# In the last group's rows, GpSimd takes the last tile's deviation ahead of the second tile's result, and VectorE finishes the third tile

## The reference

```python
y = mixed + x                                     # the experts' weighted sum, and the residual
mu = jnp.mean(y, axis=-1, keepdims=True)
var = jnp.mean(jnp.square(y - mu), axis=-1, keepdims=True)
ffn = gamma * (y - mu) * jax.lax.rsqrt(var + LN_EPS) + beta
out = _layernorm(x + ffn)                         # z = x + ffn; (z - mean) / sqrt(var + eps)
```

## Time and profile before

| | us |
|---|---|
| time, median of 3 runs | 239.36 |
| lowest and highest run | 239.25, 239.49 |
| the profiled execution's own time | 238.96 |
| its span, first to last instruction | 237.2 |
| busy in it: PE, DVE, POOL | 215.7, 182.4, 117.2 |

### The profile page before, as it was taken

The page is one execution under the profiler, slowest core; times in us unless marked ns, Lnnn a source line. Parts: engine busy times, 40 slices in busy tenths (PEclk is TensorE's granted clock), DMA queues, the critical chain, the costliest instruction groups (busy, mean ns, idle before and its releaser), DMA issues.

```text
span 237.2 us, 7191 instructions
## 1 busy us (share of the span) xinstructions
PE 215.7 (91%) x2720; PEld 184.2 (78%) x2720; DVE 182.4 (77%) x622; ACT 133.9 (56%) x221; POOL 117.2 (49%) x231
## 2 busy tenths in 40 slices
PE   7889999999999987888899999999999999999920
PEld 6767678877786665677787999789988999789920
DVE  1689999989998998465754678986889778956871
ACT  2688989999999985421479202971059400890000
POOL 5099997989998893243820400251004400221785
PEclk9999999999999999999999999999999999999995
DMA  5930543656557652200000000010000100000001
GB/s 154 276 88 12 105 66 67 142 120 131 126 112 122 136 107 65 39 5 1 0 3 0 3 0 1 0 47 0 4 0 0 46 3 1 0 22 25 0 12 33
DMA packets 32452, 12.29 MB, mean 52 GB/s; under 512 B 19906, under 2 KB 32290, under 8 KB 32418
## 3 DMA queue, kind: packets, MB, share of 16 engines
q1 hardware_dynamic: 31698, 11.54, 22.7%
q10 hardware_dynamic: 720, 0.30, 0.5%
HBM read 6.33 MB, written 1.05 MB: 31 GB/s over the span
## 4 chain that ended last, share of the span: by engine, by line
PE 68%; POOL 11%; DVE 10%; issue 7%; ACT 2%; POOLq 0%; DVEq 0%
PE score_pair L1233 12%; PE bank L1247 11%; PE scoreT_pair L1247 11%; PE scoreT_pair L1233 7%; PE bank L983 5%; PE bank L987 4%; DVE rowmax L1299 4%; PE bank L908 3%; PE scoreT_pair L940 3%; PE score_pair L924 2%; PE bank L946 2%; POOL rs L594 2%; POOL rs L479 2%; POOL x_all L585 2%; POOL w_part L504 1%
## 5 line engine op out<-in xcount | busy, mean ns | idle before, releaser
L592 POOL TENSOR_TENSOR ve<-mv,table 128x4 f32<-128x4 f32 (+2 forms) x19 | 4.7, 246 | 79.7 <-DVE mv L1652 61.1
L1299 DVE TENSOR_REDUCE rowmax<-score_pair 128x8 f32<-128x1024 f32 x32 | 38.9, 1215 | 3.0 <-PE score_pair L924 2.0
L726 ACT ACTIVATE early<-scoreT_pair 128x1024 f32<-128x1024 f32 x32 | 32.8, 1024 | 5.2 <-PE scoreT_pair L940 4.9
L1233 PE MATMUL score_pair<-x2T_part,w_part 128*128 128x512 f32 x120 | 32.0, 402 | 0.6 <-ACT x2T_part L845 0.6
L858 ACT ACTIVATE early<-score_pair,b 128x512 f32<-128x512 f32 x40 | 27.5, 688 | 4.8 <-PE score_pair L1233 4.4
L1247 PE MATMUL bank<-w,early 128*128 128x128 f32 x256 | 30.1, 276 | 0.0
L1247 PE MATMUL scoreT_pair<-w,early 128*128 128x128 f32 x256 | 29.9, 275 | 0.0
L1247 PEld LDWEIGHTS bank<-w,early 128*128 128x128 f32 x256 | 29.5, 192 | 0.3
L1247 PEld LDWEIGHTS scoreT_pair<-w,early 128*128 128x128 f32 x256 | 29.2, 192 | 0.0
L1233 PEld LDWEIGHTS score_pair<-x2T_part,w_part 128*128 128x128 f32 x120 | 21.7, 188 | 6.6 <-ACT early L858 1.4
L983 PE MATMUL bank<-early,v_pad 128*32 128x128 f32 x512 | 26.4, 278 | 0.1
(11 more groups left out here) (204 smaller groups left out, 458.5 us busy)
## 6 DMA issues: line engine op xcount, KB each, us to landing
w<-in_w SPq DMA_DIRECT2D x8, 256.0 KB, 3.4
x_ext<-in_x SPq DMA_DIRECT2D x4, 256.0 KB, 6.1
qT_all<-mT SPq DMA_DIRECT2D x32, 32.0 KB, 2.3
early<-in_xT SPq DMA_DIRECT2D x3, 256.0 KB, 4.7
early<-in_ctxT SPq DMA_DIRECT2D x3, 256.0 KB, 5.3
out<-qkv_all SPq DMA_DIRECT2D x3, 256.0 KB, 2.3
table<-in_tables SPq DMA_DIRECT2D x1, 321.0 KB
out<-qkv_all SPq DMA_DIRECT2D x4, 64.0 KB, 1.5
```

The costliest lines, as they stand in the source:

```text
L726: act.activation(prob[n % 2][:, 2 * u:2 * u + 2, :, :], scoreT_pair[:, :].rearrange("p (i j s) -> p i j s", i=2, j=QUAD), ACT.Exp, scale=S ...
L1233: mm = pe.matmul(hidden_bank[c][:, :], w1_part[:, w, c * P:(c + 1) * P], x2T_part[:, x, :], start=(k == 0), stop=(k == 2))
L1299: dve.tensor_reduce(rowmax[:, H // 2 * u:H // 2 * (u + 1)], score_pair[:, :].rearrange("p (r t) -> p r t", t=S), AX_X, ALU.max).then_inc(s ...
```

## The change

GpSimd no longer computes the result of tile 2. It computes the inverse deviations of tile 3's third norm and of tile 2's fourth norm directly behind that of tile 1's fourth norm, and only then the result of tile 1, ahead of the last inverse deviation. VectorE computes the result of tile 2, between its statistics of tile 3's `z` and the result of tile 3. SyncE waits for tile 2 on a semaphore of its own, `third_res`; the order of the stores stays.

```diff
-            res_ready""".split()
+            res_ready third_res""".split()
@@ def store(g, tiles):
                 if g == G - 1 and tiles.start == GT - 1:
                     sp.wait_ge(s["last_res"], 1)
+                elif g == G - 1 and tiles.start == GT - 2:
+                    sp.wait_ge(s["third_res"], 1)
                 else:
@@ block.gpsimd
             last_row(2)
             rows4(1)
-            last_result(1)
             rows3(3)
             rows4(2)
-            last_result(2)
+            last_result(1)
             rows4(3)
@@ def last_row(n):   (VectorE, n = 3)
                 dve.bn_aggr(mv4[:, n, :], st4[:, n, :]).then_inc(s["z_aggr"], 1)
+                dve.wait_ge(s["rs4_ready"], G + n - 1)
+                dve.tensor_scalar(res[:, G - 1, n - 1, :], z[:, n - 1, :], mv4[:, n - 1, 0:1], rs4[:, n - 1:n],
+                                  ALU.subtract, ALU.mult).then_inc(s["third_res"], 1)
                 dve.wait_ge(s["rs4_ready"], G + n)
                 dve.tensor_scalar(res[:, G - 1, n, :], z[:, n, :], mv4[:, n, 0:1], rs4[:, n:n + 1],
                                   ALU.subtract, ALU.mult).then_inc(s["last_res"], 1)
```

## The result

The changed kernel took 238.36 us, the median of 20 runs (237.82 to 240.12), against 239.47 for the kernel before in the runs beside it (20 runs, 238.69 to 240.67). The ratio is 0.9953, with a 95% interval of 0.9937 to 0.9968: faster by 0.47%, and 1.11 us between the medians. In us the interval is 0.77 to 1.51. The forecast was 1.12 us, and 238.24 us on the earlier median of 239.36. The profiled execution took 237.85 us with a span of 236.1 us; before it was 238.96 and 237.2.

The account below looks back on a forecast made before the run. GpSimd's queue ahead of the last `rs` was taken to bound the end. Gains of 0.90, 0.13 and 0.14 less 0.04 checked the -1.12 us: 239.36 - 1.12 = 238.24 us, range 238.0 to 238.75.

Parts of the forecast that it names:

- What bounds the end: Last stretch: the number of instructions in GpSimd's queue ahead of the last `rs` sets the end, not VectorE.
- The steps of the sum: GpSimd's queue laid out start to start from the `rs` at 229.91; last result's wait ends at 233.72, -1.12 us.
- the last `rs`: GpSimd, tile 3's fourth norm: predicted at 233.12, 0.31 after its `ve` instead of 0.27 because VectorE's new result runs nearby.
- The step into tile 1's result: GpSimd, from tile 2's `rs` to tile 1's result: 0.53 without a wait; 0.66 possible, up to +0.13.
- Meetings of the two engines: GpSimd and VectorE instructions side by side at the end: 0.04 charged for tile 2's result beside tile 1's; bound +0.35.
- The bound of +0.29 for tile 3's `ve` at 230.44: GpSimd's third-norm `ve` beside VectorE's `yn` at 230.50: up to +0.29 if VectorE gets ahead; zero taken.
- What the prediction said of `z`: VectorE, tile 3's `z`: runs its usual 0.35 us beside GpSimd's `ve` and `rs`, not blocked as the skill's rule says.
- The slack: Before GpSimd's last `ve`: tile 3's statistics on VectorE ready at 232.31, `ve` at 232.81, 0.50 us of cover.
- The stores: SyncE's last stores: costed at nothing; tail of 2.0 us from the last store's issue to the end stays.
- this rival: SyncE's stores queue up, each landing before the next moves: tile 3's lands +0.63 later, 239.99 us; chance 0.04.

Follow-up runs that it names:

- the last experiments: Changed kernel with tile 1's result also on VectorE: ratio 0.9942; that plus GpSimd's reordered deviations, those of tiles 1 and 2 in one call: 0.9905.
- the order alone: Against the kernel before: GpSimd computes both deviations ahead of tile 1's result, but tile 2's result stays on GpSimd; ratio 0.9969.
- the stores held together: Against the changed kernel: stores of tiles 1 to 3 all held until the last result is there; ratio to the kernel before 0.9993.
- the move alone: Against the changed kernel: GpSimd keeps its old order, tile 1's result ahead of tile 3's deviation; tile 2's result on VectorE; ratio to before 0.9975.
- joined deviations: Against the changed kernel: GpSimd does tile 3's third-norm deviation first, tiles 1 and 2's fourth-norm ones in one call; VectorE computes three last results; 237.38 us.
- both results on VectorE: Against the changed kernel: tile 1's result also moved to VectorE, between the last tile's `yn` and `z`; ratio to the kernel before 0.9942.

## Why the prediction was right

**What bounds the end.** Shown. GpSimd's queue did: one result more or less in it, with the last tile's data early, changes the end stretch by 4.38 - 3.62 = 0.76 us, which is the 0.77 of one result from start to start.

**The steps of the sum.** From the `rs` of tile 1's fourth norm (229.91 before, 229.97 after) the last result was predicted at +3.81 and came at +3.77. The steps into the `ve`s were 0.53, 0.51 and 0.77 (0.53, 0.53, 0.77 predicted), each `rs` 0.26 or 0.27 after its `ve` (0.27, and 0.31 for the last), the last result 0.60 after the last `rs` (0.60). The step into tile 1's result was 0.56, near the 0.53 taken and far from the 0.66 of one that waits: a result whose `rs` is long done starts with no gap.

**How close it came.** The step sizes are what was predicted well. That the medians differ by 1.11 us where 1.12 was forecast is partly luck: the interval reaches 0.4 us to either side, and the end stretch has 1.15. In the sum, too, misses cancel in part: -0.05 at the last `rs`, +0.03 at tile 1's result, -0.02 at a `ve`.

**Meetings of the two engines.** This is the one term that didn't come. I had charged 0.04 for VectorE's result beside GpSimd's; both ran their usual 0.35 and 0.80 us, and the `rs` came 0.26 after its `ve`. The row it was taken from the earlier trace rows was an addition with two inputs in on-chip memory, the result has one. The 0.80 us result of before didn't run beside nothing, as the prediction says, but met VectorE's statistics at 233.17 in its first 0.14 us, without effect. The bound of +0.29 for tile 3's `ve` at 230.44 wasn't touched either: it ran 0.05 us ahead of `yn` and took 0.19. What the prediction said of `z` held too: it took 0.35 us beside `ve` and `rs`, with no sign of a block. The Trainium skill, page "SBUF — State Buffer", section "Who interferes with whom", states the block for the whole instruction where VectorE works in a mode with both ports; of two inputs it says only that they contend.

**The slack.** Predicted 0.50, measured: statistics ready at 232.36, `ve` at 232.88, so 0.52. That it was real is what the last experiments show: beyond it a shorter queue brings nothing (0.44 of 0.77, then idle time).

**The stores.** Costed at nothing, and nothing it was: 2.0 us from the last issue to the end, before and after. One premise of this rival was misread: before, too, the last store had another close in front of it.

```profile
234.04 0.33 SPq L387 DMA_DIRECT2D out<-qkv_all  x1
```

That is 1.17 us ahead of the last store at 235.21, less than the 1.5 us of a landing, so by the rival's own rule the kernel before would have been held up too, to 234.04 + 3.0 = 237.04, and the loss would have been 0.30 us and not 0.63. The experiment decides it, not this row. In the changed kernel the three are issued at 232.93, 233.32 and 234.11.

**The scatter.** The size of the gain was right, but the runs scatter more widely than the first three of before (0.24 us) let one see: 2.3 us over 20 runs of the changed kernel. The part of it that I followed comes from the first 14 us. Of the nine traces two have the long matmuls of 1.51 us, the order alone and the stores held together, and these are the two whose row maximum is late (14.91 and 15.10 us; 13.43 to 14.07 in the others, where the matmuls take 0.90 to 0.93). The granted clock is given as 1.00 from 4 to 10 us in the traces with long matmuls too, so the profile shows where the time goes but not why.

## What to carry to other kernels

At the end of a program, read the last engine's queue from start to start and ask which of its instructions the last tile doesn't need; each one taken away counts in full, until the next chain is late. A better order and a shorter queue can be worth more together (1.15 us of the end stretch) than their sum (0.39 + 0.54), because the one provides the slack that the other uses. And when whole times scatter more than the effect, measure from an event just ahead of the change to one just behind it.

## What the runs showed of the hardware that was not expected

How much an instruction of one engine is held up by one of the other differs from meeting to meeting. GpSimd's result takes 0.80 us with no more than VectorE's statistics beside it, 0.94 when VectorE's `yn` (two inputs in on-chip memory) starts 0.08 us ahead of it (in the kernel before, and 0.94 again with the move alone), and 0.80 when a result of VectorE (one input) starts 0.17 us behind it, which takes its usual 0.35 as well. Kind of instruction and order of the starts differ together here, so which of them decides isn't shown. A `ve` of one column that started 0.14 us inside such a VectorE result took 0.25 instead of 0.19, with its `rs` 0.33 instead of 0.27 behind it (joined deviations); two that started 0.16 and 0.17 us inside one took 0.20 (the move alone, both results on VectorE). VectorE's `yn`, with two inputs, started 0.08 us inside an `rs` and took its usual 0.35 (joined deviations). In all these meetings the cost is 0 to 0.14 us, not the length of the other instruction. But it isn't always so small. VectorE's addition of two inputs, first with GpSimd idle and then behind GpSimd's multiplication of two inputs, in the kernel before:

```profile
150.33 0.26 DVE L1646 TENSOR_TENSOR x_ext<-x_ext,odd_sum 128x128 f32<-128x128 f32 x1
...
228.71 0.45 POOL L653 TENSOR_TENSOR yn<-yn,bias 128x128 f32<-128x128 f32 x1
228.77 0.54 DVE L1646 TENSOR_TENSOR x_ext<-x_ext,odd_sum 128x128 f32<-128x128 f32 x1
```

It lost 0.28 us and ended 0.15 us after GpSimd's instruction, as the one at 224.96 ended 0.14 after. The Trainium skill, page "SBUF — State Buffer", section "Who interferes with whom", says that the loser waits out the winner's whole instruction where VectorE works in a mode with both ports. By that, if VectorE's result used the shared ports at all, the one at 232.28 in the changed kernel would have ended after 232.91; it ended at 232.63.
